# Dense attention: some of the row maxima go through the score banks, ScalarE and GpSimd in place of VectorE

## The chip, the core and the metric

The kernel runs on one core of one Trainium2 chip. The metric is the device time of one execution in microseconds (us). Before the change the median of three runs is 5092.77 us (5092.59 to 5112.78).

## What is computed

Two transformer layers over 4096 tokens of 256 features, each with 16 heads of 16 features. Layer 0 has a block-sparse causal attention and an fp8-like product. Layer 1 has two full causal attentions over all 4096 tokens (one with rotary embedding, one with normalised queries and keys) and a mixture of four experts. The part that the change is about is the full attention, cut from the reference:

```
scores = jnp.einsum('bhqd,bhkd->bhqk', Q, K) / math.sqrt(Dh)
causal = jnp.tril(jnp.ones((T, T), dtype=bool))
scores = jnp.where(causal, scores, jnp.finfo(scores.dtype).min)
attn = jax.nn.softmax(scores, axis=-1)
y = jnp.einsum('bhqk,bhkd->bhqd', attn, V)
```

It is done twice (jobs 1 and 2 of the kernel). The softmax needs the maximum of each query's scores over all keys up to it.

## The kernel before

**Stages.** Norms and projections of layer 0; the sparse attention; a middle stage; the two dense attentions in one stage, `attend((1, 2), "dense", ...)`; at last the output projections and the experts. `attend` (L542) writes both attentions.

**Units of the dense stage.** Four heads form a group (GROUP = 4), so that there are 2 jobs x 4 groups. 512 queries are a strip, of which there are 8; a unit is one group with one query strip j, 64 units in all, j rising in one group and falling in the next. A unit's keys are taken twice.

**First pass, the tiles (row maxima).** For each key strip kc from 0 to j, each pair of heads i (0, 1), each block b of 128 queries (0 to 3) and each head of the pair, TensorE multiplies 128 queries with 512 keys into one PSUM bank (L813), and VectorE reduces the bank to one maximum per query (L951). These are 16 tiles per key strip. On the diagonal, kc = j, a tile is (b + 1) x 128 keys wide, and VectorE adds the mask while it takes the maximum (L944). The dense stage has 4608 tiles, 1024 of them diagonal. Tiles, the turned maxima ("hand") and the turned outputs ("out") share three banks in turn, 5 to 7: PE fills number e only when VectorE has freed number e - 3. After a unit's last tile VectorE joins the maxima and negates them in three small instructions (L962, L964, L966, "negate"); they are turned by TensorE, copied, and sent by SyncE to two extra rows of the queries.

**Second pass, the chunks (scores and weighing).** A chunk is 128 keys of one unit; a unit has 4(j + 1) chunks, the stage 1152. The extra rows make TensorE's product (L845, keys on the partitions, 512 queries) come out with the maximum already subtracted. Two heads fill two banks at once, a pair; there are two pairs of banks (0 and 1, 2 and 3), so the pair number i waits for ScalarE's exponential of pair i - 2. ScalarE takes the exponential of 128 x 1024 in one instruction (L908). A diagonal chunk has fewer query columns and a mask that PE adds (L777). Then PE multiplies with the values into bank 4 (L885, eight matmuls per chunk), for the chunk before the one just scored. At the end of a unit ScalarE copies bank 4 (L913).

**Order of the work.** One list, `order`, is built ahead, and every engine walks through it in order and does its own kinds of entry. Per chunk it is: tiles until `goal + 2`, the two pairs of scores, tiles until `goal + 4`, the weighing of the chunk before. So each chunk of scores has four tiles: two, the scores, two. `lead(n)` says how many chunks the tiles are ahead of the scores: 10 at the start, growing to 36; in the last eight units it is the unit's size + 4.

```
return min(max(sizes) + 4, 10 + int((2 * BLOCKS * (ends[n] - sizes[n])) ** 0.5))
...
emit_tiles(4 * (m + lead(n)) + 2)
...
emit_tiles(4 * (m + lead(n)) + (2, 4)[h // 2])
```

**GpSimd in this stage** (`attend_pool`) issues the DMAs of each group's keys and values (L683, L688), and splits expert weights into a high and a low part (L1003, L1005: gate_w, e0_up, e2_l1, e1_w1, e1_w2). The other expert weights are split by GpSimd in the last stage (L1942, L1944), each chunk loaded by SyncE into one of two staging tiles.

## Time and profile before

| | us |
|---|---|
| median of three runs | 5092.77 |
| lowest, highest | 5092.59, 5112.78 |
| span of the profiled execution | 5116.3 |
| busy in it: PE, DVE, ACT, POOL | 4781.3, 4006.1, 2867.2, 241.8 |
| groups L951 (row maxima), L944 (diagonal maxima, dense) | 2227.5, 452.4 |
| group L908 (exponentials, dense) | 2068.1 |

The profiled execution was recorded by itself; no time beside its span is shown for it. Its span is 23.5 us, or 0.46%, above the median, and 3.5 us above the slowest of the three runs. PE is TensorE (its weight loads are PEld), DVE VectorE, ACT ScalarE, POOL GpSimd, SP SyncE. A matmul's end in the profile is modelled, and matmuls overlap, so that PE looks busy where it waits within a line; starts are better to read than durations. Idle time stands in brackets behind a line, with what ended it.

### The profile page before, as it was taken

The page shows a single profiled execution, that of the slowest core. Times are in us where ns is not written, and L with a number is a line of the kernel's source. Part 1 is how long each engine was busy: PE and PEld are TensorE (multiplying, and loading weights), DVE is VectorE, ACT ScalarE, POOL GpSimd, SP SyncE. Part 2 cuts the span into 40 slices and gives each one's busy share as a digit, 9 for nine tenths or more (in the row PEclk, how much of TensorE's full clock was granted, in tenths as well). Part 3 has the DMA queues.
Part 4 walks back from the last instruction along what each step waited for, and adds up shares of the span by engine and source line. Part 5 has one row for each costly group of instructions (what it writes and reads, how often), then busy time and mean ns, then how long its engine had stood idle before and what let it go on. Part 6 is the DMA issues. An engine that isn't in the chain of part 4 may idle for free.

```text
span 5116.3 us, 82733 instructions
## 1 busy us (share of the span) xinstructions
PE 4781.3 (93%) x31872; PEld 2539.4 (50%) x31872; DVE 4006.1 (78%) x9075; ACT 2867.2 (56%) x3349; POOL 241.8 (5%) x259
## 2 busy tenths in 40 slices
PE   6699997868999999999999999999999999899999
PEld 5455555754434344433334433334443333688888
DVE  8677775767898988888888989988899875555555
ACT  4356554433566766666666667666567677332232
POOL 5200001110000000000000000000000000300000
PEclk9799898877899999999999999999899999899999
DMA  6622223765000201200300300300300000210010
GB/s 192 175 77 69 65 51 105 230 221 97 16 11 14 48 16 32 43 9 5 50 13 21 58 9 5 50 13 20 54 11 8 9 7 7 71 42 21 21 42 9
DMA packets 259185, 258.36 MB, mean 50 GB/s; under 512 B 78288, under 2 KB 198096, under 8 KB 257440
## 3 DMA queue, kind: packets, MB, share of 16 engines
q1 hardware_dynamic: 250784, 212.86, 14.8%
q0 software_dynamic: 6240, 38.80, 4.7%
q8 instruction: 251, 4.11, 0.3%
q10 hardware_dynamic: 1768, 1.42, 0.2%
q14 instruction: 142, 1.16, 0.1%
HBM read 145.44 MB, written 105.97 MB: 49 GB/s over the span
## 4 chain that ended last, share of the span: by engine, by line
PE 73%; DVE 19%; issue 5%; ACT 2%; SPq 1%; DMA 1%; DVEq 0%; ACTq 0%
PE psum L885 24%; PE psum L813 20%; PE psum L76 14%; DVE maxes_dense L951 11%; PE psum L845 4%; PE psum L777 3%; PE psum L802 2%; PE psum L823 1%; PE psum L854 1%; PE psum L1656 1%; DVE masked_scores_dense L944 1%; PE psum L809 1%; PE psum L1636 0%; PE psum L864 0%; ACT probs_dense L908 0%
## 5 line engine op out<-in xcount | busy, mean ns | idle before, releaser
L908 ACT ACTIVATE probs_dense<-psum 128x1024 f32<-128x1024 f32 (+3 forms) x2304 | 2068.1, 950 | 1042.2 <-PE psum L845 755.1
L951 DVE TENSOR_REDUCE maxes_dense<-psum 128x1 f32<-128x512 f32 x3584 | 2227.5, 684 | 232.1 <-PE psum L813 231.3
L813 PE MATMUL psum<-keys,queries_dense 48*128 48x512 f32 (+3 forms) x4608 | 1553.0, 477 | 114.6 <-DVE maxes_dense L951 22.1
L813 PEld LDWEIGHTS psum<-keys,queries_dense 48*128 48x128 f32 x4608 | 668.2, 191 | 1471.4 <-DVE maxes_dense L951 1143.6
L885 PE MATMUL psum<-probs_dense,values 128*32 128x512 f32 (+3 forms) x9216 | 1181.2, 591 | 0.0
L845 PE MATMUL psum<-queries_dense,keys 50*128 50x512 f32 (+3 forms) x4608 | 809.7, 407 | 11.5 <-ACT probs_dense L908 11.2
L944 DVE CUSTOM_DVE_ANT_0 masked_scores_dense<-psum,causal_add 128x128 f32<-128x128 f32 (+3 forms) x1024 | 452.4, 488 | 151.5 <-PE psum L813 132.2
L845 PEld LDWEIGHTS psum<-queries_dense,keys 50*128 50x128 f32 x4608 | 449.6, 193 | 106.4 <-ACT probs_dense L908 60.0
L944 DVE CUSTOM_DVE_ANT_0 masked_scores_sparse<-psum,after_add 128x512 f32<-128x512 f32 x512 | 326.2, 687 | 99.9 <-PE psum L802 99.0
L1763 ACT ACTIVATE activated<-psum 128x512 f32<-128x512 f32 x208 | 124.4, 598 | 417.5 <-PE psum L76 405.8
L885 PEld LDWEIGHTS psum<-probs_dense,values 128*32 128x32 f32 x9216 | 189.9, 109 | 273.1 <-issue 203.0
L908 ACT ACTIVATE probs_sparse<-psum 128x1024 f32<-128x1024 f32 x224 | 217.7, 1022 | 147.2 <-PE psum L777 59.7
L802 PE MATMUL psum<-str_keys,queries_sparse 48*128 48x512 f32 x512 | 179.6, 513 | 48.3 <-DMA own_values<-v_scratch 25.8
L1898 DVE CAST hid_high<-activated 128x512 fp32r<-128x512 f32 x208 | 91.9, 442 | 143.5 <-ACT activated L1763 140.7
L1900 DVE TENSOR_TENSOR hid_low<-activated,hid_high 128x512 fp32r<-128x512 f32 x208 | 150.4, 723 | 7.2
L802 PEld LDWEIGHTS psum<-str_keys,queries_sparse 48*128 48x128 f32 x512 | 72.2, 195 | 168.2 <-DVE maxes_sparse L944 88.8
L885 PE MATMUL psum<-probs_sparse,str_values 128*32 128x512 f32 x1024 | 148.7, 655 | 0.0
L777 PE MATMUL psum<-tri_key,eye_bf 64*128 64x128 bf16 x2048 | 147.3, 223 | 0.0
L908 ACT ACTIVATE probs_sparse<-psum,after_bias 128x1024 f32<-128x1024 f32 x96 | 101.6, 1111 | 67.0 <-PE psum L854 67.0
L854 PE MATMUL psum<-queries_sparse,str_keys 50*128 50x512 f32 x512 | 127.3, 462 | 1.6 <-ACT probs_sparse L908 1.6
L948 DVE TENSOR_REDUCE maxes_sparse<-psum 128x4 f32<-128x512 f32 x128 | 83.7, 689 | 53.3 <-PE psum L809 51.7
L1912 DVE SCALAR_TENSOR_TENSOR xa_s<-psum,wts,xa_s 128x192 f32<-128x192 f32 x128 | 52.8, 416 | 81.6 <-PE psum L76 80.8
(296 smaller groups left out, 5252.6 us busy)
## 6 DMA issues: line engine op xcount, KB each, us to landing
v_scratch<-ve_s SPq DMA_DIRECT2D x96, 256.0 KB, 3.5
queries_dense<-parts_scratch SPq DMA_DIRECT2D x384, 64.0 KB
keys<-parts_scratch POOLq DMA_DIRECT2D x42, 512.0 KB, 18.0
parts_scratch<-part_high SPq DMA_DIRECT2D x16, 1024.0 KB, 4.3
parts_scratch<-part_low SPq DMA_DIRECT2D x16, 1024.0 KB, 7.1
values<-v_scratch POOLq DMA_DIRECT2D x8, 2048.0 KB, 35.3
queries_sparse<-parts_scratch SPq DMA_DIRECT2D x192, 64.0 KB
own_keys<-parts_scratch SPq DMA_DIRECT2D x192, 64.0 KB
```

Of the source, the lines that this page charges most:

```text
L76: m = pe.matmul(out_ap, left(l, c), right(r, c), start=(n == 0), stop=(n == len(pairs) - 1))
L777: m = pe.matmul(bank, eye2[own, part, :], addend, start=start and part == 0, stop=stop and part == 1)
L802: m = pe.matmul(bank, q[rows(h, TROWS), h // 2, b * P:(b + 1) * P], str_keys[n // STRIPS][rows(h, TROWS), h // 2, :], start=True, stop=True)
L813: m = pe.matmul(bank[:, 0:width], q[rows(h, TROWS), h // 2, b * P:(b + 1) * P], k[rows(h, TROWS), h // 2, kc * STRIP:kc * STRIP + width], ...
L845: m = pe.matmul(full[:, first_col:STRIP], k[own, h // 2, c * P:(c + 1) * P], q[own, h // 2, first_col:STRIP], start=True, stop=not diagonal)
L854: m = pe.matmul(full, str_keys[n // STRIPS][own, h // 2, c * P:(c + 1) * P], q[own, h // 2, :], start=True, stop=not partly)
L885: m = pe.matmul(psum[own_rows, 4, cols], vt, probs[(2 * m_at + h // 2) % 6][:, h % 2, cols], start=(c == 0), stop=(c == sizes[n] - 1 and b ...
L908: act.activation(probs[i % 6][:, :, first_col:STRIP], psum[:, at2:at2 + 2, first_col:STRIP], ACT.Exp, scale=SCALE, **extra).then_inc(exp_d ...
L944: m = dve.tensor_tensor_reduce(out=masked_scores[e % 2][:, 0:width], in0=bank[:, 0:width], in1=mask, scale=1.0, scalar=-3e38, op0=ALU.add, ...
L951: m = dve.tensor_reduce(mx[:, h * BLOCKS + b, kc:kc + 1], bank, AX.X, ALU.max)
L1763: act.activation(gs[k % 2][:], h_bank(u), func).then_inc(activated, 1)
L1900: dve.tensor_tensor(low[:, f, :], g[:], high[:, f, :].bitcast(F32), ALU.subtract).then_inc(hid_split, 1)
```

## The change

- `copied_pairs`: in the units with j of 2 or more, the two tiles of pair i = 1, block b = 3 of each key strip off the diagonal are taken out of the tiles. In their place a "copy" entry stands in the middle of the strip's tiles.
- For a copy PE fills one pair of the score banks, and ScalarE copies it to SBUF: for kc = 0 to one of two `runs` tiles, otherwise to one of two `copies` tiles. The turn of the two pairs of banks now goes over copies and scores together (`ring_at`).
- For kc of 1 and more GpSimd takes run = run + max(copy - run, 0) in three instructions ("merge"), each waiting for the one before.
- After the unit's last tile VectorE waits for the last merge and reduces the run of 128 x 1024 to two maxima ("fold"), before the negation.
- The tiles are no longer spread as four per chunk: the list `FOUR` gives the goals before, between and behind the scores of four chunks in turn, and a copy counts as two. Off the diagonal with a copy that makes 3, 3, 5 and the copy, and 3 tiles; in a strip without a copy 3, 3, 7, 3. `lead` becomes a multiple of four.
- ScalarE and GpSimd walk through `order` too. GpSimd's loads and splits come at the units' starts. VectorE sets all maxima to -3e38 once.
- The splits of e1_w1 and e1_w2 move from the dense stage to the head of the last stage's list, and PE's first wait for them there goes by the later one.

```diff
-            return [(kc, 2 * i + odd, b) for kc in range(j + 1) for i in range(PAIRS) for b in range(BLOCKS) for odd in range(2)]
+            return [(kc, 2 * i + odd, b) for kc in range(j + 1) for i in range(PAIRS) for b in range(BLOCKS) for odd in range(2)
+                    if kc == j or (i, b) not in copied_pairs(n)]
+
+        def copied_pairs(n):
+            if sparse or units[n][2] < 2:
+                return ()
+            return ((1, BLOCKS - 1),)
+
+        def steps_of(n):
+            steps = [("tile", n, tile) for tile in tiles_of(n)]
+            pairs = copied_pairs(n)
+            per_strip = GROUP * BLOCKS - 2 * len(pairs)
+            for kc in reversed(range(units[n][2] if pairs else 0)):
+                for p in reversed(range(len(pairs))):
+                    at = kc * per_strip + (per_strip * (2 * p + 1)) // (2 * len(pairs))
+                    steps.insert(at, ("copy", n, (kc, *pairs[p])))
+            return steps
...
-            return min(max(sizes) + 4, 10 + int((2 * BLOCKS * (ends[n] - sizes[n])) ** 0.5))
+            return min(max(sizes) + 4, 4 * int(3 + (2 * BLOCKS * (ends[n] - sizes[n])) ** 0.5 / 4))
...
+                before, made = made, made + (2 if kind == "copy" else 1)
...
+                if made == 4 * ends[n]:
+                    for p in range(len(copied_pairs(n))):
+                        order.append(("fold", n, p))
                     order.append(("negate", n, None))
...
+        FOUR = ((2, 3, 3), (4, 6, 6), (10, 12, 13), (15, 15, 16))
...
-                emit_tiles(4 * (m + lead(n)) + 2)
+                goals = [4 * (m + lead(n)) + more for more in (2, 2, 4)]
+                if not sparse:
+                    goals = [4 * (m - c % 4 + lead(n)) + more for more in FOUR[c % 4]]
+                emit_tiles(goals[0])
                 for h in range(GROUP):
...
-                        emit_tiles(4 * (m + lead(n)) + (2, 4)[h // 2])
+                        emit_tiles(goals[1 + h // 2])
...
+                def wait_pair(r):
+                    if r >= 2:
+                        name, count = pair_users[r - 2]
+                        pe.wait_ge(copied if name == "copied" else exp_done, count)
...
+                    elif kind == "copy":
+                        kc, i, b = what
+                        r = ring_at["copied", copy_at[n, what] + 1]
+                        wait_pair(r)
+                        for odd in range(2):
+                            m = pe.matmul(psum[:, 2 * (r % 2) + odd, :], q[rows(odd, TROWS), i, b * P:(b + 1) * P],
+                                          k[rows(odd, TROWS), i, kc * STRIP:(kc + 1) * STRIP], start=True, stop=True)
+                        m.then_inc(copy_filled, 1)
...
+                    elif kind == "copy":
+                        kc, i, b = what
+                        x = copy_at[n, what]
+                        at2 = 2 * (ring_at["copied", x + 1] % 2)
+                        act.wait_ge(copy_filled, x + 1)
+                        if kc == 0:
...
+                            target = runs[run % 2]
+                        else:
+                            y = merge_at[n, what]
+                            if y >= 2:
+                                act.wait_ge(merged, y - 1)
+                            target = copies[y % 2]
+                        act.activation(target[:], psum[:, at2:at2 + 2, :], ACT.Copy).then_inc(copied, 1)
...
+                    elif kind == "fold":
+                        i, b = copied_pairs(n)[what]
+                        run = run_at[n, (i, b)]
+                        dve.wait_ge(merged, merge_at[n, (units[n][2] - 1, i, b)] + 1)
+                        chain.then(dve.tensor_reduce(maxes[n % 2][:].rearrange("p (h o b) s -> p h o b s", o=2, b=BLOCKS)[:, i, :, b, 0],
+                                          runs[run % 2][:], AX.X, ALU.max))
...
+                    elif kind == "copy" and what[0] >= 1:
+                        kc, i, b = what
+                        run, y = runs[run_at[n, (i, b)] % 2], merge_at[n, what]
+                        copy = copies[y % 2]
+                        pool.wait_ge(copied, copy_at[n, what] + 1)
+                        if y >= 1:
+                            pool.wait_ge(merged, y)
+                        pool_chain.then(pool.tensor_tensor(copy[:], copy[:], run[:], ALU.subtract))
+                        pool_chain.settle()
+                        pool_chain.then(pool.tensor_scalar(copy[:], copy[:], 0.0, None, ALU.max))
+                        pool_chain.settle()
+                        pool.tensor_tensor(run[:], run[:], copy[:], ALU.add).then_inc(merged, 1)
...
-        chunk for name, n_out in (("gate_w", EXPERTS), ("e0_up", HID), ("e2_l1", HID), ("e1_w1", HID), ("e1_w2", HID))
+        chunk for name, n_out in (("gate_w", EXPERTS), ("e0_up", HID), ("e2_l1", HID))
...
-                ("e0_down", HID, DIM, MASKED), ("e2_l2", HID, HID, 0), ("e1_down", HID, DIM, MASKED), ("e3_down", DIM, DIM, 0),
+                ("e1_w1", DIM, HID, 0), ("e1_w2", DIM, HID, 0), ("e0_down", HID, DIM, MASKED), ("e2_l2", HID, HID, 0), ("e1_down", HID, DIM, MASKED), ("e3_down", DIM, DIM, 0),
...
-                    pe.wait_ge(late_split, late_ready[name])
+                    pe.wait_ge(late_split, late_ready[gate or name])
```

## Rows read from the trace of the kernel before

**Rows 1.** The page's part 1, whole execution.
```profile
PE 4781.3 (93%) x31872; PEld 2539.4 (50%) x31872; DVE 4006.1 (78%) x9075; ACT 2867.2 (56%) x3349; POOL 241.8 (5%) x259
```

**Rows 2.** Busy time by stretch, dense stage: PE, PEld, DVE, ACT, POOL, clock, DMA.
```profile
1150.00:4362.00 3212.00, 3101.52 (x20789) 1283.25 (x20787) 2757.32 (x5994) 2105.43 (x2368) 49.76 (x70) 0.95 0.13 25
```

**Rows 3.** Timeline, one chunk in mid-stage: start us, us, engine, line, what, [idle before].
```profile
2503.40 0.50 PE L813 MATMUL psum<-keys,queries_dense 48*128 48x512 f32 x2
...
2503.74 0.63 PE L845 MATMUL psum<-queries_dense,keys 50*128 50x512 f32 x4
2503.94 2.48 DVE L951 TENSOR_REDUCE maxes_dense<-psum 128x1 f32<-128x512 f32 x4 [0.64 <-PE psum L813]
...
2504.18 1.94 ACT L908 ACTIVATE probs_dense<-psum 128x1024 f32<-128x1024 f32 x2 [0.95 <-PE psum L845]
2504.21 0.97 PE L813 MATMUL psum<-keys,queries_dense 48*128 48x512 f32 x2
2504.68 0.18 PEld L813 LDWEIGHTS psum<-keys,queries_dense 48*128 48x128 f32 x1 [0.52 <-DVE maxes_dense L951]
...
2505.11 1.07 PE L885 MATMUL psum<-probs_dense,values 128*32 128x512 f32 x8
...
2506.11 0.50 PE L813 MATMUL psum<-keys,queries_dense 48*128 48x512 f32 x2
```

**Rows 4.** The chain that ended last, the same chunk: start us, us, what.
```profile
2503.47 0.48 PE psum L813 x2
2503.95 0.69 DVE maxes_dense L951
...
2504.68 0.50 PE psum L813
```

**Rows 5.** Groups of instructions by form, 1800 to 4000 us.
```profile
L951 DVE TENSOR_REDUCE maxes_dense<-psum 128x1 f32<-128x512 f32 x2503 | 1556.9, 684 | 156.9 <-PE psum L813 156.4
L908 ACT ACTIVATE probs_dense<-psum 128x1024 f32<-128x1024 f32 x1338 | 1296.8, 1021 | 529.0 <-PE psum L845 490.3 <-PE psum L777 33.5
```

**Rows 6.** The chain where PE waits for nothing: start us, us, what.
```profile
2487.95 0.26 PE psum L813 x2
2488.21 0.52 PE psum L845 x4
...
2488.98 0.99 PE psum L885 x8
```

**Rows 7.** Timeline of PE, a diagonal strip's four chunks: the weighings.
```profile
2486.89 1.06 PE L885 MATMUL psum<-probs_dense,values 128*32 128x512 f32 x8
...
2488.91 1.06 PE L885 MATMUL psum<-probs_dense,values 128*32 128x512 f32 x8
...
2495.96 1.06 PE L885 MATMUL psum<-probs_dense,values 128*32 128x512 f32 x8
...
2499.10 1.06 PE L885 MATMUL psum<-probs_dense,values 128*32 128x512 f32 x8
```

**Rows 8.** Groups of GpSimd by form, whole execution.
```profile
L518 POOL TENSOR_TENSOR x_in<-x_in,y_s 128x512 f32<-128x512 f32 x16 | 27.1, 1691 | 1.3
...
L1005 POOL TENSOR_TENSOR e_w_low<-stage,e_w_high 128x512 fp32r<-128x512 f32 x4 | 5.1, 1271 | 0.3
...
L1005 POOL TENSOR_TENSOR w_moe_qkv_low<-stage,w_moe_qkv_high 128x768 fp32r<-128x768 f32 x2 | 3.7, 1830 | 0.2
...
L1003 POOL CAST w_moe_qkv_high<-stage 128x768 fp32r<-128x768 f32 x2 | 1.7, 826 | 38.1 <-DMA stage<-in_moe_qkv 38.1
```

**Rows 9.** Line L951 while GpSimd works, 1468.3 to 1470.3 us: duration ns min/median/max.
```profile
L951 DVE TENSOR_REDUCE maxes_dense<-psum x5: 681/682/692, 1467.7 to 1470.2; 128x1 f32<-128x512 f32 x5
```

**Rows 10.** Timeline of the last stage: a GpSimd split, and PE's first use of e_w.
```profile
4382.62 1.26 POOL L1944 TENSOR_TENSOR e_l_low<-stage,e_l_high 128x512 fp32r<-128x512 f32 x1
...
4408.47 0.39 PE L76 MATMUL psum<-xft_high,e_w_high 128*128 128x512 f32 x1
```

More of the change, by code:

```diff
@@ L623, in attend @@
         order.append(("out", len(units) - 1, None))
+        pair_users, copy_at, run_at, run_units, merge_at = [], {}, {}, [], {}
+        for kind, n, what in order:
+            if kind == "copy":
+                kc, i, b = what
+                copy_at[n, what] = len(copy_at)
+                if kc == 0:
+                    run_at[n, (i, b)] = len(run_at)
+                    run_units.append(n)
+                else:
+                    merge_at[n, what] = len(merge_at)
+                pair_users.append(("copied", copy_at[n, what] + 1))
+            elif kind == "score" and what[2] % 2 == 1:
+                pair_users.append(("exp_done", 2 * what[0] + what[2] // 2 + 1))
+        ring_at = {user: r for r, user in enumerate(pair_users)}
         side_at = {}
@@ L667, in attend @@
                 tri_key2 = sbuf(st, "tri_key2", [P, 2, P], BF16)
+                runs = [sbuf(st, f"max_runs_{i}", [P, 2, STRIP]) for i in range(2)]
+                copies = [sbuf(st, f"max_copies_{i}", [P, 2, STRIP]) for i in range(2)]
                 halves = ((eye2, "c_ident_bf"), (tri_key2, "c_tri_key"))
@@ L782, in attend_pe @@
                 for kind, n, what in order:
-                    if kind not in ("tile", "hand", "out", "unit", "score", "weigh"):
+                    if kind not in ("tile", "copy", "hand", "out", "unit", "score", "weigh"):
                         continue
@@ L895, in attend_act @@
                     act.wait_ge(bias_set, 1)
-                for n, (a, g, j) in enumerate(units):
-                    for c in range(sizes[n]):
-                        m_at = ends[n] - sizes[n] + c
+                for kind, n, what in order:
+                    a, g, j = units[n] if n < len(units) else (None, None, None)
+                    if kind == "score" and what[2] % 2 == 1:
+                        m_at, c, h = what
                         first_col = 0 if sparse else max(0, c - BLOCKS * j) * P
@@ L901, in attend_act @@
                         extra = {"bias": after_bias[:, 0:1]} if hidden else {}
-                        for half in range(2):
-                            i = 2 * m_at + half
-                            at2 = 2 * (i % 2)
-                            act.wait_ge(scored, i + 1)
-                            if i >= 6 and half == 0:
-                                act.wait_ge(weighed, m_at - 2)
-                            act.activation(probs[i % 6][:, :, first_col:STRIP], psum[:, at2:at2 + 2, first_col:STRIP],
-                                           ACT.Exp, scale=SCALE, **extra).then_inc(exp_done, 1)
@@ L922, in attend_dve @@
                 else:
+                    for tile in maxes:
+                        chain.then(dve.memset(tile[:], -3e38))
                     chain.then(dve.memset(causal_add[:], 0.0))
@@ L994, in load, with split @@
                     load_values(pool, group)
-                if not sparse:
-                    pool.wait_ge(queries_in[1], count_loaded(1))
-                    load_values(pool, 0)
-                    load(1)
-                for i, (src, high, low) in enumerate(chunks):
+                def split(i):
+                    src, high, low = chunks[i]
                     part = tiles[i % 2][:, 0:high.shape[1]]
@@ L1006, in attend_pool @@
                 if not sparse:
-                    for group in range(2, len(groups)):
-                        load(group)
+                    pool.wait_ge(queries_in[1], count_loaded(1))
+                    load_values(pool, 0)
+                for kind, n, what in order:
+                    if kind == "unit":
+                        if n < len(chunks):
+                            split(n)
+                        if not sparse and n == 1:
+                            load(1)
+                        if not sparse and n % STRIPS == 0 and 2 <= n // STRIPS + 1 < len(groups):
+                            load(n // STRIPS + 1)
+                    elif kind == "copy" and what[0] >= 1:
+                        kc, i, b = what
+                        run, y = runs[run_at[n, (i, b)] % 2], merge_at[n, what]
[8 more added lines that the diff above has]
+                        pool.tensor_tensor(run[:], run[:], copy[:], ALU.add).then_inc(merged, 1)
             attend_sp()
```

55 lines of the change are left out of this document (35 added, 20 removed).

## The prediction

> **What bounds the kernel now.** I read the busy shares first: PE 93%, VectorE 78%, ScalarE 56%, GpSimd 5% [rows 1]. Then the dense stage alone, 3212 us of the span: PE 3102, VectorE 2757 (86%), ScalarE 2105 (66%), GpSimd 50 [rows 2]. By these PE is the bound, but its ends are modelled, so I went to the timeline of one chunk [rows 3] and to the chain [rows 4]. A chunk in mid-stage takes 2.71 us: from the tiles' start at 2503.40 to the next at 2506.11. In it VectorE works 2.48 and is idle 0.23. PE issues two tiles, two pairs of scores and the third tile, and only at 2504.68 the fourth: its bank is free when VectorE has reduced the chunk's first tile. The loop that closes is: first tile filled 0.48, reduced 0.69, fourth tile 0.50, weighing 1.00, and the next first tile behind it. Where VectorE's tiles are narrow, the chain has PE alone: 0.26 for two tiles, 0.52 for two pairs of scores, 0.99 for the weighing [rows 6], and a chunk takes 2.02 us by the starts of two weighings [rows 7]. So PE's own floor is about 2.03 per chunk, VectorE's 2.48, and the loop through both costs the last 0.23.
>
> **Part 1, two of 16 tiles leave VectorE.** Units with j of 2 to 7 have 2 + 3 + 4 + 5 + 6 + 7 = 27 key strips off the diagonal per group, 216 in eight groups. That is 432 of 3584 reduces of 684 ns [rows 5]; by spacing one costs (2.48 - 0.68) / 3 = 0.60. A strip is four chunks, 10.8 us now, with 16 x 0.60 = 9.6 of VectorE. Afterwards:
> - VectorE 14 x 0.60 = 8.4.
> - ScalarE 8 exponentials and a copy. Two exponentials take 1.94, one 1.02, so the spacing is 0.92, and a copy of the same 1024 columns is put at the same: 9 x 0.92 = 8.3.
> - PE multiplies as much as before, but single tiles no longer share their time with a neighbour on the other half of the rows. I count slots of 0.26 (two neighbours or one alone): 4, 4, 6 and 4 in the four chunks, 18 x 0.26 + 4 x 0.99 = 8.6.
>
> The three engines are within 4% of each other, so their order decides. I walked through four chunks with these durations, a tile being ready for VectorE 0.54 after its start and its bank free 0.74 after VectorE's start, both as in [rows 3]. The tiles themselves hardly wait: three banks carry VectorE over the weighing. Two waits are left on PE. In the second chunk the second pair of scores waits 0.2 for the exponential two turns before. In the third the copy has taken a turn of the banks, and the second pair of scores waits 0.5 for ScalarE to end it. The walk gives 9.2. A matmul that has waited shows its weight load too: the fourth tile held the weighing off for 0.43 (2504.68 to 2505.11) against a slot of 0.26, so 0.17 for each of two waits; I take 9.4. That saves 1.4 per strip: 216 x 1.4 = 302 us. Bounds: 9.2 with nothing beside the walk (346), and 9.9 if each chunk loses over PE's floor as much as VectorE loses in one now, with the two weight loads on top: 8.6 + 4 x 0.23 + 0.34 (194).
>
> **Part 2, the uneven spread where nothing is copied.** 64 diagonal strips and the 8 of j = 1 have 16 tiles in 3, 3, 7, 3. A diagonal strip takes now 9.07 (2486.89 to 2495.96 [rows 7]), mostly at PE's floor. With seven tiles in the third chunk, two of them 512 wide in front, VectorE has about 3.8 in that chunk while the others fall back to 2.0: 2.0 + 2.0 + 3.8 + 2.1 = 9.9. So +0.8 each, +51 us; bounds +0.4 (the next chunk absorbs half) and +1.1.
>
> **Part 3, the folds.** 48 reductions of 128 x 1024 from SBUF on VectorE. No row has one; the nearest is 684 ns for 512 columns, of which 0.60 is spacing, so 1.2 is the estimate and 0 to 1.4 the bounds. It stands just before the negation, where VectorE is late already: the chunk behind it takes 3.14 (2495.96 to 2499.10 [rows 7]) in place of 2.71. PE has three banks of cover, so I take 1.0 of it: 48 us, bounds 0 and 60.
>
> **Part 4, GpSimd's merges.** (j - 1) summed over j = 2 to 7 is 21 per group: 168 merges of three instructions. The subtraction of two inputs took 1271 ns for 512 columns and 1830 for 768, so 2.4 for 1024; the one-input form 826 for 768 columns, so about 1.05 [rows 8]. A merge is 2.4 + 1.05 + 2.4 = 5.9 us. It lies beside a strip of 9.4 us, and a copy waits only for the merge before the last, so nothing waits: 0. The slowest two-input row, 1691 for 512 columns, would make a merge 6.8 + 1.05 = 7.9, still under 9.4. The DMA issues and the splits that now stand in GpSimd's queue between merges are within the 50 us of [rows 2], once per group or unit, and the keys they load are needed some hundred chunks later: 0. If that cover went, a load's few us would stand in front of one copy per group. SyncE's queue is passed by nothing new.
>
> **Part 5, e1_w1 and e1_w2 split late.** Four more splits stand at the head of the last stage. The split that now ends at 4383.88 (4382.62 + 1.26) is the sixth of that list, and PE uses e_w first at 4408.47 [rows 10]. The four new ones are earlier in the list, so 25 us of cover: 0 (bounds 0 and +9, four times about 2 us, if something behind them is waited for).
>
> **The sum.** -302 + 51 + 48 = -203. From the profiled span of 5116.3 that is 4913; from the median, which is 23.5 lower, 4890. A second way: VectorE keeps its share. Its work falls by 432 x 0.60 = 259 and rises by 58, net -201 of 2757; at 86% that is -234, so 4859. I keep the first.
>
> **Rivals.**
> 1. **The turn of the banks costs more.** ScalarE at 8.3 and PE at 8.6 of every strip leave no slack, and what the walk treats as two short waits may be four. For it: ScalarE is waited for already in a stage where it is 66% busy, and it is in order. Against it: exponentials were idle 529 us before their start in 1800 to 4000 us, waiting for PE [rows 5]. With a strip of 10.2, the saving is 130 less 99: about 5060 us.
> 2. **VectorE is the only thing that counted.** PE's single tiles cost nothing extra and folds hide: a strip of 9.1, 367 - 26 - 10 = 331: 4762 us.
> 3. **Slower: GpSimd's merges hold VectorE up.** Both work in SBUF at once for the first time in this stage over long stretches, 168 x 5.9 = 990 us. If VectorE stood still for a share of that, it would be on the bound. It decides from 203 / 168 = 1.2 us per merge; at a third of each merge, 2.0, it costs 336 and the time is 5226; at all of it 5881. Against it: while GpSimd did a one-input and a two-input instruction, five reduces around them took 681 to 692 ns [rows 9], the same as the mean.
> 4. **The change moves nothing:** the loop finds another closure at 10.6 per strip: 43 saved against the 99 of parts 2 and 3, 56 slower, near 5150. This needs VectorE idle over 2 us in a strip, and I see no such wait.
>
> To rival 3 the Trainium skill, "Perfetto Trace Analysis", section "Optimizing Scalar/DVE Operations", says that VectorE and GpSimd share an SBUF read port, so moving work between them might not help. By that page taken at its word, the time would be rival 3's. "SBUF — State Buffer", section "Who interferes with whom", narrows it: a VectorE instruction with at most one SBUF input outside the two-port modes does not contend. The trace agrees with the narrower one, with its 681 to 692 ns.
>
> **How the numbers follow.** Forecast (strips of 9.2 to 9.9 with the bounds of parts 2 and 3) 0.62; rival 1 0.15; rival 2 0.10; rival 3 0.06; rival 4 0.03; smaller slips to about no change 0.04. A measurement can tell about 0.5% of this time, 25 us, from no change; rival 1, with its strips at 10.0 to 10.4, lies for two thirds on the faster side of it. Faster 0.62 + 0.10 + 0.10 = 0.82, the same 0.05 + 0.04 = 0.09, slower 0.06 + 0.03 = 0.09. The range: the forecast's own bounds are -346 + 26 + 0 = -320 and -194 + 70 + 60 = -64, so 4773 to 5029; I cut the upper end to 5010, which keeps the better part of rival 1's faster half, and set the low end to 4775.
>
> **What would show it.** Right: the dense stage near 3010 us; reduces x3152; between two copies of a big unit about 9.4 us; VectorE over 88% busy in mid-stage; ScalarE's copies x216 near 1.0 us; merges of about 5.9 us with GpSimd idle between them; reduces still 684 ns; PE's waits for probs (L908) or copies up from nearly nothing, once or twice per strip; folds near 1.2. Wrong: a copy-to-copy distance over 10.2; reduces over 0.75 us while GpSimd works; copies on ScalarE waiting for merges; waits of PE for the late splits.

## The result, and the profile after

| | before | changed |
|---|---|---|
| median, 20 runs each (us) | 5095.66 | 5084.62 |
| lowest, highest (us) | 5071.83, 5122.38 | 5032.10, 5110.35 |
| ratio, 95% interval | | 0.9957, 0.9937 to 0.9976 |
| the same, second chip job (12 and 23 runs) | 5106.58 | 5074.99; 0.9935, 0.9908 to 0.9962 |
| span of the profiled execution (us) | 5116.3 | 5057.5 |

By the two ratios the change makes the kernel faster by 0.4% to 0.7%, 22 to 33 us, where 203 us were forecast and the range began at 83 us. The sign was right, the size was not. The ratio is taken over fast runs and leaves out the one of 5110.35 us, so it is not that of the medians in the table, which lie 11 us apart in the first job and 32 us in the second.

The page of the changed kernel, part 1 and the groups that answer to [rows 1, 5, 8] (out<-in, count | busy us, mean ns | idle before, releaser):

```profile
PE 4677.8 (92%) x31872; PEld 2510.8 (50%) x31872; DVE 3799.2 (75%) x8693; ACT 3077.2 (61%) x3565; POOL 1508.0 (30%) x763
...
L965 ACT ACTIVATE probs_dense<-psum 128x1024 f32<-128x1024 f32 (+3 forms) x2304 | 2078.8, 952 | 638.7 <-PE psum L902 393.3
L1029 DVE TENSOR_REDUCE maxes_dense<-psum 128x1 f32<-128x512 f32 x3152 | 1960.0, 683 | 347.1 <-PE psum L863 344.7
...
L1107 POOL TENSOR_TENSOR max_copies<-max_copies,max_runs 128x1024 f32<-128x1024 f32 x168 | 399.5, 2378 | 1639.1 <-ACT max_copies L982 1639.1
...
L1109 POOL TENSOR_SCALAR max_copies<-max_copies 128x1024 f32<-128x1024 f32 x168 | 464.7, 2766 | 14.8
L1111 POOL TENSOR_TENSOR max_runs<-max_runs,max_copies 128x1024 f32<-128x1024 f32 x168 | 400.0, 2381 | 14.0
...
L982 ACT ACTIVATE max_copies<-psum 128x1024 f32<-128x1024 f32 x168 | 172.1, 1024 | 102.5 <-PE psum L871 102.5
```

And the busy time of the stretch of [rows 2], in the same columns:

```profile
1150.00:4362.00 3212.00, 3040.23 (x20953) 1288.82 (x20953) 2573.37 (x5634) 2331.12 (x2605) 1342.98 (x610) 0.94 0.13 26
```

The work went where the change sent it. VectorE has 184 us less in this stretch (2757 to 2573), ScalarE 226 more, GpSimd 1343 in place of 50; the dense stage ends some 60 us earlier, so that the stretch now holds the beginning of the last stage too. But VectorE's tiles now wait for PE: 347 us before L1029, where L951 had 232 before the change. VectorE's share of the stretch fell from 86% to 80%, where over 88% in mid-stage had been named as the sign of being right. The profiled execution ran at a mean granted clock of 0.931, and the median of the first twenty runs is 0.925.

Four chunks of a strip with a copy, at the full clock. The lines are those of the timeline with the starts of the weighings (L942) and what PE waits for in the copy's chunk (L871 is the copy's fill, L902 scores, L863 tiles, L982 ScalarE's copy):

```profile
2421.95 1.06 PE L942 MATMUL psum<-probs_dense,values 128*32 128x512 f32 x8
...
2424.09 1.06 PE L942 MATMUL psum<-probs_dense,values 128*32 128x512 f32 x8
...
2426.22 1.07 PE L942 MATMUL psum<-probs_dense,values 128*32 128x512 f32 x8
...
2427.22 0.72 PE L871 MATMUL psum<-keys,queries_dense 48*128 48x512 f32 x2
...
2427.84 0.19 PEld L902 LDWEIGHTS psum<-queries_dense,keys 50*128 50x128 f32 x2 [0.33 <-ACT probs_dense L965]
...
2427.99 1.02 ACT L982 ACTIVATE max_copies<-psum 128x1024 f32<-128x1024 f32 x1 [0.20 <-PE psum L871]
...
2428.49 0.18 PEld L863 LDWEIGHTS psum<-keys,queries_dense 48*128 48x128 f32 x1 [0.35 <-DVE maxes_dense L1029]
2428.91 1.94 ACT L965 ACTIVATE probs_dense<-psum 128x1024 f32<-128x1024 f32 x2
2429.07 0.19 PEld L902 LDWEIGHTS psum<-queries_dense,keys 50*128 50x128 f32 x2 [0.39 <-ACT max_copies L982]
...
2429.73 1.07 PE L942 MATMUL psum<-probs_dense,values 128*32 128x512 f32 x8
...
2431.86 0.64 PE L942 MATMUL psum<-probs_dense,values 128*32 128x512 f32 x4
```

Three chunks take 2.14, 2.13 and 2.13 us (2421.95, 2424.09, 2426.22, and behind the copy's chunk 2429.73 to 2431.86). The copy's chunk takes 3.51. Together 9.91 where it was 10.8; over some 100 such strips of this trace that ran at the full clock throughout, the median is 9.88. In the copy's chunk PE's loads wait three times: 0.33 for an exponential, 0.35 for VectorE, 0.39 for ScalarE's copy. These are the waits for ScalarE in the list of waits, 1800 to 4000 us (waiting engine, for whom: us in total, times, longest):

```profile
PEld psum L902 <- ACT probs_dense L965: 49.5, 165, 0.7
...
PEld psum L902 <- ACT max_copies L982: 46.7, 120, 0.4
```

### The profile page after: what moved, and what is told of

It reads as the page before. It is cut to its first block and busy times, and to the rows that moved or that the text cites. A ratio compares the mean times of both kernels' runs of the same rounds, so it can differ in the third digit from the quotient of the medians.

```text
span 5057.5 us, 83460 instructions
## 1 busy us (share of the span) xinstructions
PE 4677.8 (92%) x31872; PEld 2510.8 (50%) x31872; DVE 3799.2 (75%) x8693; ACT 3077.2 (61%) x3565; POOL 1508.0 (30%) x763
## 3 DMA queue, kind: packets, MB, share of 16 engines
q14 instruction: 149, 1.22, 0.1%
## 5 line engine op out<-in xcount | busy, mean ns | idle before, releaser
L1029 DVE TENSOR_REDUCE maxes_dense<-psum 128x1 f32<-128x512 f32 x3152 | 1960.0, 683 | 347.1 <-PE psum L863 344.7
L863 PE MATMUL psum<-keys,queries_dense 48*128 48x512 f32 (+3 forms) x4176 | 1446.0, 459 | 130.3 <-DVE maxes_dense L1022 46.7
L863 PEld LDWEIGHTS psum<-keys,queries_dense 48*128 48x128 f32 x4176 | 651.4, 193 | 1255.3 <-DVE maxes_dense L1029 800.5
L942 PE MATMUL psum<-probs_dense,values 128*32 128x512 f32 (+3 forms) x9216 | 1188.2, 594 | 0.0
L902 PE MATMUL psum<-queries_dense,keys 50*128 50x512 f32 (+3 forms) x4608 | 1082.3, 434 | 35.2 <-ACT probs_dense L965 14.2
L1107 POOL TENSOR_TENSOR max_copies<-max_copies,max_runs 128x1024 f32<-128x1024 f32 x168 | 399.5, 2378 | 1639.1 <-ACT max_copies L982 1639.1
L902 PEld LDWEIGHTS psum<-queries_dense,keys 50*128 50x128 f32 x4608 | 515.3, 194 | 249.2 <-ACT probs_dense L965 104.0
L1109 POOL TENSOR_SCALAR max_copies<-max_copies 128x1024 f32<-128x1024 f32 x168 | 464.7, 2766 | 14.8
L1111 POOL TENSOR_TENSOR max_runs<-max_runs,max_copies 128x1024 f32<-128x1024 f32 x168 | 400.0, 2381 | 14.0
L942 PEld LDWEIGHTS psum<-probs_dense,values 128*32 128x32 f32 x9216 | 190.3, 110 | 325.7 <-issue 273.7
L982 ACT ACTIVATE max_copies<-psum 128x1024 f32<-128x1024 f32 x168 | 172.1, 1024 | 102.5 <-PE psum L871 102.5
L821 PE MATMUL psum<-tri_key,eye_bf 64*128 64x128 bf16 x2048 | 183.8, 228 | 0.0
L871 PE MATMUL psum<-keys,queries_dense 48*128 48x512 f32 x432 | 167.2, 472 | 0.0
```

The source lines that it names most:

```text
L821: m = pe.matmul(bank, eye2[own, part, :], addend, start=start and part == 0, stop=stop and part == 1)
L863: m = pe.matmul(bank[:, 0:width], q[rows(h, TROWS), h // 2, b * P:(b + 1) * P], k[rows(h, TROWS), h // 2, kc * STRIP:kc * STRIP + width], ...
L902: m = pe.matmul(full[:, first_col:STRIP], k[own, h // 2, c * P:(c + 1) * P], q[own, h // 2, first_col:STRIP], start=True, stop=not diagonal)
L942: m = pe.matmul(psum[own_rows, 4, cols], vt, probs[(2 * m_at + h // 2) % 6][:, h % 2, cols], start=(c == 0), stop=(c == sizes[n] - 1 and b ...
L1029: m = dve.tensor_reduce(mx[:, h * BLOCKS + b, kc:kc + 1], bank, AX.X, ALU.max)
L1107: pool_chain.then(pool.tensor_tensor(copy[:], copy[:], run[:], ALU.subtract))
```

## The experiments

Two theories. **A**: the gain per strip was over-sized, and the rest of the sum is right. **B**: something takes back a gain that is there, and it is TensorE's granted clock. What spoke for B at first were the changed kernel's own runs: of the first twenty, one at a mean granted clock of 0.939 took 5032.10 us, one at 0.922 took 5105.25, 4.3 us for each 0.001. In c1 below it is 5040.83 at 0.937 and 5110.90 at 0.919, 3.9 for each; I use 4.1, an estimate. A straight line through all runs gives 4.0 in the first job and 3.5 in c1's. The code is the same in all of them.

All runs, with the ratio to the kernel before on the same chip and the median of the mean granted clock over the kernel's runs. The kernel before has 0.936 in each of these jobs; its clocks in the job of the first twenty runs are not on record.

| run | ratio | 95% interval | clock |
|---|---|---|---|
| c1, the changed kernel | 0.9935 | 0.9908 to 0.9962 | 0.930 |
| e1, even spread where nothing is copied | 0.9838 | 0.9808 to 0.9868 | 0.933 |
| e2, no copies, even spread | 1.0005 | 0.9978 to 1.0032 | 0.939 |
| e3, no copies, uneven spread | 1.0983 | 1.0924 to 1.1042 | 0.850 |
| e4, the fold twice | 1.0235 | 1.0188 to 1.0282 | 0.902 |
| e5, longer merges | 0.9958 | 0.9924 to 0.9991 | 0.926 |
| e6, longer copies | 1.0734 | 1.0662 to 1.0807 | 0.869 |
| e7, copies with the old spread | 1.0345 | 1.0308 to 1.0382 | 0.902 |
| e8, e1 and an earlier fold | 0.9693 | 0.9659 to 0.9727 | 0.944 |
| f1, the earlier fold alone | 0.9859 | 0.9831 to 0.9887 | 0.934 |
| f2, e8 with the fold earlier still | 0.9751 | 0.9718 to 0.9785 | 0.944 |
| f3, e8 with a tile moved | 0.9705 | 0.9675 to 0.9735 | 0.944 |
| g1, e3 with seven tiles filled twice | 1.0712 | 1.0657 to 1.0766 | 0.904 |
| g2, changed kernel, PE kept busy behind the fold | 0.9946 | 0.9916 to 0.9976 | 0.936 |

**c1, the changed kernel once more.**

> The changed kernel, unchanged, on this chip beside the others and with the clock of each run. Theory A (the gain per strip was over-sized: 9.9 us where 9.4 was forecast; the diagonal strips and folds cost what was forecast): ratio to before 0.994 to 0.998 again. Theory B (TensorE's clock: its granted clock is lower than in the kernel before, and takes back a gain of some 100 us that is there at full clock): the mean granted clock of the runs is below 0.93 where the kernel before has 0.934, and the time falls by some 4 to 5 us for each 0.001 of clock.

Both held in part: the ratio lies just under A's range and the clock on B's bound. The clock is 0.930 in the median of twelve runs against 0.936. At the same clock the kernels can be set side by side: at 0.933 the changed kernel took 5060.16 and 5064.01, the kernel before 5119.72 and 5121.60. So 59 us are gained at the same clock, and the lower clock takes back 0.006 x 4.1 us per 0.001 = 25 us of it here; in the first twenty runs, with a median of 0.925, probably more. Theory B is right in kind, and too large: 59 are not 203.

**e1, the even spread where nothing is copied; f1, the earlier fold; e8, both; f2, earlier still.**

```diff
+        with_copy = [len(copied_pairs(n)) > 0 and kc < units[n][2] for n in range(len(units)) for kc in range(units[n][2] + 1)]
...
-                if not sparse:
+                strip = (m - c % 4 + lead(n)) // 4
+                if not sparse and (strip >= len(with_copy) or with_copy[strip]):
                     goals = [4 * (m - c % 4 + lead(n)) + more for more in FOUR[c % 4]]
```

```diff
-                if made == 4 * ends[n]:
+                if made == 4 * ends[n] - 4:
                     for p in range(len(copied_pairs(n))):
                         order.append(("fold", n, p))
+                if made == 4 * ends[n]:
                     order.append(("negate", n, None))
```

The first is e1, the second f1, both together e8; f2 has 8 in place of the 4.

> As the changed kernel, but tile strips without a copy (64 diagonal ones and the 8 of j = 1) are spread 4, 4, 4, 4 again. Theory A: diagonal strips fall from 9.86 to 9.1 us, 64 x 0.78 = 50 us under the changed kernel, ratio to before 0.986. Rival (the seven-tile chunk costs nothing in sum, the next chunks absorb it): ratio as of the changed kernel, 0.996.

> The changed kernel with the fold four tiles earlier, and the uneven spread everywhere. Theory A+B (the fold ahead of the negation costs TensorE about 0.8 us per unit at full clock, and the wait starts stretches at the lower clock): 60 to 75 us under the changed kernel, as between e1 and e8, with a mean granted clock over 0.93: ratio 0.980 to 0.983. Theory A alone: 38 us, ratio 0.987, with the clock as it was.

> As e1, and the fold stands four tiles before the end of the diagonal strip, where VectorE waits for narrow tiles, in place of just before the negation. Theory A: the 1.1 us per unit that fold and negation cost together falls by about 0.8, 48 x 0.8 = 38 us under e1, ratio to before 0.979. Rival (the wait is GpSimd's last merge, 7.5 us long, which is then not done): no gain over e1, or a loss.

> As e8, and the fold eight tiles before the end. GpSimd's last merge ends 3 x 2.5 us after its copy is in SBUF, so about 9 us after the copy's fill; eight tiles before the end is about 10 us after it. Theory A: same as e8, ratio 0.969, or a little slower where the merge is late. Rival (the merge is late there, VectorE waits for GpSimd): 1 us or more per unit back, ratio over 0.975.

e1 is 0.0097 under c1 in the same job, 50 us, which is A's number, but the clock rose by 0.003, worth 12. At 0.933 in both, e1's 5022.50 and 5021.71 are 40 us under the changed kernel's. The trace has the same: a diagonal strip at the full clock takes 9.25 us in e1 in place of 9.85, 64 x 0.6 = 38 us; its first chunk now takes 2.19 where it took 2.02 before the change. f1 is 0.0076 under c1, 39 us. That is A's number and not the 60 to 75, but some 16 of it are again the 0.004 of clock that it has more. Together they are worth more than apart: e8 is 0.0145 under e1, 74 us, and its clock is 0.944 against 0.933. At 4.1 us per 0.001 the clock holds 45 of the 74, and the fold's new place the other 29, where 38 were expected. f2 is slower than e8 by 0.6%, at e8's clock (another chip, and the intervals just touch). That is the rival's number, but not its mechanism: VectorE's list of waits, first e8's, then f2's, has none for GpSimd.

```profile
DVE masked_scores_dense L1025 <- PE psum L866: 64.0, 127, 1.0
```

```profile
DVE masked_scores_dense L1025 <- PE psum L866: 93.4, 154, 0.9
```

The reduces of the diagonal tiles (L1025) wait 29 us longer for PE. The starts of the weighings at the full clock show where each place of the fold costs. Just ahead of the negation it is the chunk in which the maxima are turned: 3.98 us in the changed kernel and 4.02 in e1, against 2.93 in e3, which has no fold. In e8 that chunk is back at 2.96, and the fourth chunk of the diagonal strip takes 2.83 in place of 2.52. In f2 it is the third, with the narrow tiles (128 and 256 keys) behind the fold, that takes 2.92 in place of 2.02. Over the end of a unit e8 has 0.75 us less than e1 (48 x 0.75 = 36 us), and f2 0.57 more than e8: 48 x 0.57 = 27 us, as much as f2 is slower.

e8's stretch from 1500 to 4000 us, below the changed kernel's in the same columns, and its fold:

```profile
1500.00:4000.00 2500.00, 2401.07 (x16911) 1004.20 (x16907) 2083.87 (x4562) 1894.29 (x2108) 1073.74 (x460) 0.96 0.13 25
```

```profile
1500.00:4000.00 2500.00, 2442.67 (x17508) 1000.95 (x17504) 2141.38 (x4688) 1962.05 (x2189) 1116.19 (x476) 0.98 0.13 25
```

```profile
L1038 DVE TENSOR_REDUCE maxes_dense<-max_runs 128x2 f32<-128x1024 f32 x40 | 48.7, 1217 | 0.0
```

In the same 2500 us e8 gets through 17508 matmuls where the changed kernel gets through 16911, at a clock of 0.98 against 0.96. The fold takes as long as ever (1217 ns). What it costs depends on where it stands.

**e2, no copies and the old spread.**

```diff
-            return ((1, BLOCKS - 1),)
+            return ()
...
-                if not sparse:
-                    goals = [4 * (m - c % 4 + lead(n)) + more for more in FOUR[c % 4]]
```

> No copies, folds or merges, and the old spread of two, scores, two: what is left of the change is the engines' walk through the one list, lead in steps of four, and e1_w1 and e1_w2 split in the last stage. Theory A: nothing, ratio 0.998 to 1.002. Rival (the late splits or the new order cost some of the gain): ratio over 1.004.

No difference, as A had it. The walk of all engines through one list, the new lead and the late splits of e1_w1 and e1_w2 cost nothing that these runs can tell, within the 0.3% of the interval. The stretch from 1500 to 4000 us:

```profile
1500.00:4000.00 2500.00, 2426.68 (x16674) 1004.10 (x16666) 2221.20 (x4806) 1696.86 (x1903) 28.17 (x42) 0.98 0.13 24
```

**e3, the uneven spread alone.** Only the first edit of e2.

> No copies, but the spread 3, 3, 7, 3 in every strip. Theory A: 64 diagonal strips + 0.8 us and 224 strips off the diagonal at 4.5 + 3 x 2.1 = 10.8 to 10.9 in place of 10.8, so + 50 to + 75 us, ratio 1.010 to 1.015. Rival (an uneven spread costs nothing in sum): 1.000.

1.0983, at a clock of 0.850: by far the largest miss. The timeline of a strip's third chunk at the full clock:

```profile
2647.42 1.07 PE L942 MATMUL psum<-probs_dense,values 128*32 128x512 f32 x8
...
2649.70 0.49 PE L863 MATMUL psum<-keys,queries_dense 48*128 48x512 f32 x1 [0.44 <-DVE maxes_dense L1029]
...
2651.91 0.64 PE L942 MATMUL psum<-probs_dense,values 128*32 128x512 f32 x4
```

4.49 us, and beside it three of 2.1, so 10.9 a strip, just as expected (10.87 in the median at the full clock, 10.80 in e2). PE waits in this chunk for VectorE at one tile after another. What was not expected is the clock: 0.086 lower, which at 4.1 us per 0.001 is 350 us, and at the 4.8 of the kernel before (5070.97 at 0.944, 5137.95 at 0.930) 410, out of the 502 that it is slower. That leaves 90 to 150 us for the strips, where 50 to 75 were expected. Part of the difference is that a strip whose tiles run beside the scores of a diagonal takes 11.21 us where it took 10.59, 42 x 0.6 = 26 us that were not counted. e2 and e3 have the same instructions in another order, so the order alone brought the clock from 0.939 to 0.850.

**g1, the same with PE's waits filled.** The seven tiles of the third chunk, off the diagonal, are multiplied twice each into the same bank.

```diff
-                            m = pe.matmul(bank[:, 0:width], q[rows(h, TROWS), h // 2, b * P:(b + 1) * P],
-                                          k[rows(h, TROWS), h // 2, kc * STRIP:kc * STRIP + width], start=True, stop=True)
+                            place = tiles_of(n).index(what)
+                            for _ in range(2 if 6 <= place % 16 <= 12 and kc < j else 1):
+                                m = pe.matmul(bank[:, 0:width], q[rows(h, TROWS), h // 2, b * P:(b + 1) * P],
+                                              k[rows(h, TROWS), h // 2, kc * STRIP:kc * STRIP + width], start=True, stop=True)
```

> The kernel without copies and with the spread 3, 3, 7, 3 in every strip (ratio 1.098 at a granted clock of 0.851), in which PE fills each of the seven tiles off the diagonal twice into the same bank: more work for PE, in the gaps where it waits for VectorE. Theory B (gaps of PE behind its waits bring the granted clock down, and that, not the waits, made 1.012 into 1.098): the clock rises above 0.90 and the time falls by over 100 us, ratio under 1.07. Rival (PE's load or the waits themselves make the time; the low clock is a consequence of neither): same or slower, ratio 1.098 or over, clock 0.85.

The same stretch, first e3, then g1 (the clock is the third number from the right; e2 has 0.98):

```profile
1500.00:4000.00 2500.00, 2364.76 (x14160) 979.59 (x14152) 1893.87 (x4133) 1459.18 (x1611) 28.16 (x42) 0.82 0.12 21
```

```profile
1500.00:4000.00 2500.00, 2399.32 (x16074) 1090.02 (x16066) 1992.51 (x4340) 1533.57 (x1699) 28.17 (x42) 0.92 0.13 24
```

More work for PE, and 151 us less time (5617.39 to 5466.40), with the clock up from 0.850 to 0.904. VectorE, whose work is the same, gets 4340 instructions done in the stretch in place of 4133. At the full clock g1 is the slower program: its seven-tile chunk takes 4.96 us in place of 4.50. It is faster in sum because less of it runs at the lower clock. So the waits of PE lower its clock, and here that costs more than the waits do. The time missed the expected 1.07 by a little: the doubled tiles are not free.

**g2, the changed kernel with PE kept busy behind the fold.** The same edit in the changed kernel, three times for the second to sixth tile of each unit from the second on.

> The changed kernel in which PE fills the second to sixth tile of each unit three times each into the same bank, about where it waits for fold and negation. Theory B: the clock rises by 0.003 to 0.008 over the changed kernel's 0.925 to 0.929 and the time falls by 10 to 30 us, ratio 0.988 to 0.993. Rival (that wait has nothing to do with the clock; PE only has more to do): 64 x 10 x 0.25 = 160 us more work, of which some shows: ratio over 1.00.

The clock rose as theory B had it, 0.930 to 0.936, but the time did not fall to 0.988 to 0.993: it is that of the changed kernel (0.9946 beside 0.9935). If the clock gave what it gives elsewhere, the extra matmuls took it. It neither proves the price of the clock nor speaks against it.

**e4, the fold twice.** The fold's instruction is issued a second time behind the first.

> The fold is done twice. Theory A (VectorE is the bound behind the negation, so its time counts nearly in full): 48 x 1.25 = 60 us over the changed kernel, ratio 1.008. Rival (three banks of cover hide it): under 20 us more, ratio below 1.000.

1.0235, 0.030 over c1, 153 us where 60 were expected. The clock fell by 0.028, worth some 115 at 4.1 per 0.001; the rest, 40, is less than the 58 that 48 more reductions of 1.2 us can cost. The trace has the same 40: at the full clock the end of a unit takes 0.84 us more than in the changed kernel (18.27 and 17.43 for the same six chunks), and 48 x 0.84 = 40. A's 60 was too much by a third, and the clock did the rest.

**e5, longer merges.** One more instruction on GpSimd in each merge, and no other edit.

```diff
+                        pool_chain.then(pool.tensor_scalar(copy[:, 0, :], copy[:, 0, :], 0.0, None, ALU.max))
+                        pool_chain.settle()
                         pool.tensor_tensor(run[:], run[:], copy[:], ALU.add).then_inc(merged, 1)
```

> Each merge has one more GpSimd instruction of 512 columns (about 1.5 us; a merge is then 9 us). Theory A (GpSimd is off the path): no change to the changed kernel within 0.3%. Rival (GpSimd's merges hold up ScalarE's copies or VectorE): up to 168 x 1.5 = 250 us more.

From its groups, 1500 to 4000 us:

```profile
L1029 DVE TENSOR_REDUCE maxes_dense<-psum 128x1 f32<-128x512 f32 x2571 | 1599.9, 683 | 269.0 <-PE psum L863 267.3
...
L1111 POOL TENSOR_SCALAR max_copies<-max_copies 128x512 f32<-128x512 f32 x139 | 206.7, 1487 | 11.5
```

168 x 1.49 = 250 us more on GpSimd, and no change that can be told (0.9958 beside 0.9935, within the expected 0.3%, intervals overlapping). A merge of 9.0 us still fits. The reduces take 683 ns with GpSimd at work in about half of the time.

**e6, longer copies.** ScalarE copies half of each copy's columns once more ahead of the copy, and the counts that PE and GpSimd wait for rise with it.

```diff
-                        act.activation(target[:], psum[:, at2:at2 + 2, :], ACT.Copy).then_inc(copied, 1)
+                        act.activation(target[:, :, 0:2 * P], psum[:, at2:at2 + 2, 0:2 * P], ACT.Copy).then_inc(copied, 1)
+                        act.wait_ge(copied, 2 * x + 1)
+                        act.activation(target[:], psum[:, at2:at2 + 2, :], ACT.Copy).then_inc(copied, 1)
```

> ScalarE copies half of each copy's columns once more before the copy, 0.6 to 0.75 us per copy in the turn of the score banks. Theory A (in the copy's chunk PE waits for ScalarE: 3.51 us where TensorE and the walk ask for 3.0): the chunk grows by nearly all of it, 216 x 0.6 = 130 us or more over the changed kernel, ratio 1.02. Rival (VectorE's tiles set the copy's chunk, ScalarE has room): under 40 us more, ratio below 1.004.

```profile
L982 ACT ACTIVATE max_copies<-psum 128x512 f32<-128x512 f32 x120 | 71.7, 597 | 93.2 <-PE psum L871 93.2
```

The extra copy takes 597 ns, and by the starts of the weighings the copy's chunk takes 4.14 us at the full clock in place of 3.51: 0.63 more, all of it. So ScalarE's part in the turn of the banks ends last in that chunk. In sum it is 1.0734, 400 us over the changed kernel, of which 216 x 0.63 = 136 are the copies; the clock is 0.869, and 0.061 under c1's is worth another 250.

**e7, the copies with the old spread.** Only the second edit of e2.

> The changed kernel's copies and folds with the spread of before (two, scores, two; a copy counts as two and falls behind the scores of a chunk, just ahead of its weighing). Theory A (the turn of the score banks sets the copy's chunk; copies right behind two pairs of scores wait for an exponential): a strip with a copy about 10.3 to 10.6 us in place of 9.9, diagonal strips 9.1, so 90 to 150 us less 50 over the changed kernel, ratio to before 1.00 to 1.02. Rival (VectorE's load alone counts, the order doesn't matter): ratio of e1, 0.984.

Outside the expected 1.00 to 1.02, mostly by the clock: 0.902 against 0.936 is 140 us or more of the 176 that it is slower than before. But the strip missed as well. One with a copy, at the full clock:

```profile
2285.01 1.07 PE L940 MATMUL psum<-probs_dense,values 128*32 128x512 f32 x8
...
2287.86 0.50 PE L869 MATMUL psum<-keys,queries_dense 48*128 48x512 f32 x2 [0.65 <-ACT probs_dense L963]
2288.29 1.07 PE L940 MATMUL psum<-probs_dense,values 128*32 128x512 f32 x8
...
2290.42 1.06 PE L940 MATMUL psum<-probs_dense,values 128*32 128x512 f32 x8
...
2293.12 1.07 PE L940 MATMUL psum<-probs_dense,values 128*32 128x512 f32 x8
...
2295.83 1.06 PE L940 MATMUL psum<-probs_dense,values 128*32 128x512 f32 x8
```

That is 10.82 us (10.81 in the median at the full clock), the 10.8 of the kernel before and not 10.3 to 10.6: two reduces in sixteen have left VectorE and the strip gained nothing, since the copy's fill (L869) waits 0.65 us for an exponential. So the order decides whether the copies save anything at all; with the uneven spread the strip takes 9.88. The rival (the order doesn't matter) is out. Why the clock is lower here than in c1, whose spread is the less even one, is not shown.

**f3, one tile ahead of the scores.** e8 with (10, 13, 13) for the third chunk.

> As e8, and in the copy's chunk the fifth tile stands ahead of the second pair of scores, in PE's wait for ScalarE, in place of behind it. Theory A (PE waits there for ScalarE to end the copy): the copy's chunk falls from 3.51 to about 3.4 us, 216 x 0.1 = 20 us under e8, ratio 0.965. Rival (the tile then waits for its bank, that is for VectorE, and holds the scores): 3.5 to 3.8, ratio 0.969 to 0.98.

No gain: 0.9705 beside e8's 0.9693. By the weighings the copy's chunk stays at 3.53 at the full clock. So the rival's number came in. That the tile waits for its bank there as long as the scores had waited for ScalarE is its explanation, and no line here shows it.

## Why the prediction was wrong

**The step that failed** is part 1, "I take 9.4" for a strip with a copy, which measured 9.9. Behind it stands a term that the sum does not have: the clock was taken to stay as it is.

1. **A strip with a copy: 9.9 in place of 9.4.** 216 x 0.9 = 194 us in place of 302; this is 108 of the miss. Of the 108, 30 are a slip in adding: 9.2 and twice 0.17 make 9.54, not 9.4 (272 us and not 302). The floor under the walk was wrong too. I counted a chunk at 0.26 per slot and 0.99 for the weighing from [rows 6], 2.03 us; but those tiles are 128 and 256 keys wide (the first half of a diagonal strip), and narrow tiles cost PE less. With full tiles a chunk in which PE does not wait for VectorE takes 2.13. And the copy's chunk has 0.96 over its floor of 2.55 (six slots and the weighing), where the walk had 0.67 (0.5 and 0.17): three waits, not one. e6 shows that the turn of the banks, ScalarE's end, sets it. My own upper bound for the strip was 9.9, so the bound held and the value did not.
2. **The diagonal strips: right.** 9.85 by the weighings in place of 9.08 (9.07 in [rows 7]), + 0.8; e1 gave 50 us back, 40 of them at the same clock. "Mostly at PE's floor" was read too kindly: two of the four chunks before took 2.02 us, the other two 2.52.
3. **The folds: right.** One takes 1.22 us, and the chunk in which the maxima are turned grew by 1.05 us at the full clock (2.93 in e3, 3.98 here), where 1.0 was put.
4. **GpSimd at nothing: right, by a wrong number.** A merge takes 7.5 us, not 5.9: 2378 and 2381 ns for the two-input instructions, as forecast, but 2766 for the one with a scalar, where 1.05 us were taken from a cast: another operation in place of the one that would run. It still fits, and e5 shows room up to 9.0. Rival 3 is out. The trace agrees with the Trainium skill, "SBUF — State Buffer", section "Who interferes with whom": the reduces, which read no SBUF, take 683 ns with GpSimd busy in 30% of the span and 684 without.
5. **The late splits and the new walk at nothing: right** (e2).
6. **The sum with the measured strip** is -194 + 51 + 48 = -95. At the same clock 59 us were measured. Of the 36 between them the trace settles 25. In 42 of the 216 strips the tiles run beside the scores of a diagonal, which have fewer columns and give PE and ScalarE less to do. Such a strip took 10.59 us before and takes 10.28 now, so it saves 0.3 and not 0.9. The other 11 stay open.
7. **The clock was missing.** A lower one takes back 25 us in the second job, an estimate by the 4.1 us per 0.001; for the first job it can't be told, as the clocks of the kernel before are not on record. The changed kernel at the end of a diagonal strip shows the pattern. First the windows, in the columns of [rows 2]:

```profile
2427.20:2437.00 9.80, 9.72 (x70) 3.72 (x66) 7.53 (x21) 8.76 (x10) 7.54 (x3) 1.00 0.00 0
2437.00:2440.00 3.00, 2.26 (x15) 1.27 (x19) 2.51 (x13) 1.65 (x3) 0.00 (x0) 0.99 0.00 0
2440.00:2446.70 6.70, 6.70 (x30) 2.60 (x22) 4.95 (x16) 3.11 (x4) 0.00 (x0) 0.50 0.01 2
```

Then the timeline in and behind them:

```profile
2436.93 0.55 PE L863 MATMUL psum<-keys,queries_dense 48*128 48x512 f32 x3
...
2438.22 0.32 PE L863 MATMUL psum<-keys,queries_dense 48*128 48x128 f32 x1 [0.73 <-DVE maxes_dense L1022]
...
2439.65 1.72 PE L942 MATMUL psum<-probs_dense,values 128*32 128x512 f32 x8
...
2443.19 1.93 PE L942 MATMUL psum<-probs_dense,values 128*32 128x512 f32 x8
...
2443.92 1.22 DVE L1035 TENSOR_REDUCE maxes_dense<-max_runs 128x2 f32<-128x1024 f32 x1
```

Up to 2437 PE is busy throughout, with a clock of 1.00. From 2437 to 2440 it waits for VectorE with the tiles in front of the seven-tile chunk (0.73 us before one matmul) and is busy 2.26 of 3.00. Then 6.7 us at 0.50, that is at 1.2 GHz in place of 2.4: a weighing takes 1.72 and 1.93 where it takes 1.06. That one such wait comes ahead of a drop shows nothing by itself; what shows it are e2 and e3, where the order alone took the clock down, and g1, where filling the waits of e3 brought the clock up and the time down. The Trainium skill, "TensorE: Matmul & The Clock Gate", section "What's actually happening", says that a monitor sets the clock by how busy the array is. The runs agree, with 0.850 for the kernel whose PE waits at seven tiles in a row, 0.904 with the same waits filled, and 0.944 for the fastest.

What pattern of waits brings the clock down, and how far, is open: these runs show single cases and no rule. So the kernel before was steadier than I gave it credit for. Its loop waits a little in every chunk, and the changed kernel gathers waits in one chunk of four and at the unit's end.

The rivals: rival 1 (the turn of the banks costs more) is what came in, in a milder form, a strip of 9.9 and not 10.2; its 5060 us are nearest to what was measured. That nearness is luck: 5060 was worked out for 10.2 and an unchanged clock, and the measured strip with an unchanged clock gives 5093 - 95 = 4998. Rival 2 (a strip of 9.1) and rival 4 (10.6) are out.

**A version that beats both.** e8 keeps the copies, spreads evenly where nothing is copied, and folds four tiles earlier: 4947.98 us, ratio 0.9693 (0.9659 to 0.9727), computing the same as the kernel before.

## What to carry to other kernels

Read an engine's floor from instructions of the shape that will run, not from the stretch where it happens to wait least: here the narrow tiles of the diagonal made PE look 5% faster. When work is moved off an engine, the place of the waits matters as well as their sum; waits of TensorE gathered in one place can lower its clock and cost more than they last (e2 against e3). Compare runs at the same mean granted clock before judging a small difference, and put a new instruction where its engine idles anyway.

## What was not expected of the hardware

- The mean granted clock of the same program varies from 0.918 to 0.939 over its runs, and its time with it, 5118.13 to 5032.10 us.
- The same instructions in another order (e2 and e3) took 5105.33 and 5617.39 us, at a mean granted clock of 0.939 and 0.850.
- More matmuls made a kernel faster: 5617.39 to 5466.40 us, with seven tiles of sixteen filled twice in the strips off the diagonal.
- On GpSimd a maximum with a scalar over 128 x 1024 took 2766 ns, longer than a subtraction of two such tiles (2378).
